# Grouped attention: the values' products move to the last three steps of a tile, copy and join to the next tile's first step, output jobs to two steps behind

## The reference

```python
h = _rms(x, ln_w)
q = (h @ wq).reshape(B, S, 32, 64)          # B*S = 1024 rows in x, causal over all of S
k = (h @ wk).reshape(B, S, 8, 64)
v = (h @ wv).reshape(B, S, 8, 64)
q, k = _rope(q, k)
k, v = jnp.repeat(k, 4, axis=2), jnp.repeat(v, 4, axis=2)
scores = jnp.einsum('bqhd,bkhd->bhqk', q, k) / np.sqrt(64)
attn = jax.nn.softmax(jnp.where(causal, scores, -1e30), -1)
o = jnp.einsum('bhqk,bkhd->bqhd', attn, v).reshape(B, S, 2048)
x = x + o @ wo
```

## Time and profile before

| | |
|---|---|
| median of 3 runs | 3767.97 us (3765.26 to 3775.60) |
| profiled execution | 3772.04 us, span 3770.1 us |
| PE busy | 3251.6 us, 86% |
| DVE busy | 2463.5 us, 65% |
| ACT busy | 1971.1 us, 52% |
| POOL busy | 1694.2 us, 45% |
| layer 0 attention, first scores to the load of its output rows | 107 to 380 us |
| layer 2 attentions, first scores to the final addition L1793 | 1028 to 1698 us, 2459 to 3130 us |

### The profile page before, as it was taken

The page is one execution under the profiler, slowest core; times in us unless marked ns, Lnnn a source line. Parts: engine busy times, 40 slices in busy tenths (PEclk is TensorE's granted clock), DMA queues, the critical chain, the costliest instruction groups (busy, mean ns, idle before and its releaser), DMA issues. The chain is left out here.

```text
span 3770.1 us, 55139 instructions
## 1 busy us (share of the span) xinstructions
PE 3251.6 (86%) x16736; PEld 2534.8 (67%) x16736; DVE 2463.5 (65%) x4877; ACT 1971.1 (52%) x3957; POOL 1694.2 (45%) x1293
## 2 busy tenths in 40 slices
PE   5788698479898989988995999788889988998988
PEld 4566576148566666666883899656666666886767
DVE  4687554965577878875557565378778885555554
ACT  3787433333376767764333333277667774334333
POOL 1676221742366667752212544377666762221111
PEclk8899899889899999999998999899999999999989
DMA  2000231333201111103320000110111103332132
GB/s 76 24 31 2 77 110 61 130 103 116 62 22 28 30 30 29 27 4 122 110 80 26 1 1 1 35 33 25 26 29 32 30 7 101 109 103 93 64 98 73
DMA packets 81187, 204.07 MB, mean 54 GB/s; under 512 B 17179, under 2 KB 20379, under 8 KB 80662
## 3 DMA queue, kind: packets, MB, share of 16 engines
q1 hardware_dynamic: 80774, 200.74, 17.1%
q10 hardware_dynamic: 144, 0.07, 0.0%
HBM read 170.86 MB, written 4.69 MB: 47 GB/s over the span
## 5 line engine op out<-in xcount | busy, mean ns | idle before, releaser
L1253 POOL TENSOR_TENSOR probs<-probs,row_inverse 128x640 f32<-128x640 f32 (+7 forms) x640 | 738.9, 1159 | 485.5 <-DVE row_inverse L1279 474.3
L541 PE MATMUL psUp<-xnT_part,weights_part 128*128 128x512 f32 x3456 | 834.8, 391 | 3.3 <-DVE hidden L694 2.5
L541 PEld LDWEIGHTS psUp<-xnT_part,weights_part 128*128 128x128 f32 x3456 | 651.6, 189 | 141.6 <-POOL weights_part L515 3.3
L518 POOL TENSOR_TENSOR weights_part<-weights,weights_part 128x768 fp32r<-128x768 f32 x136 | 250.9, 1848 | 1010.9 <-ACT weights_part L597 1010.9
L1267 DVE TENSOR_REDUCE neg_max<-psS 128x1 f32<-128x640 f32 (+7 forms) x640 | 476.7, 745 | 134.4 <-PE psS L1157 133.8
L1220 ACT ACTIVATE probs<-psS,neg_max 128x640 f32<-128x640 f32 (+7 forms) x640 | 475.5, 743 | 142.5 <-DVE neg_max L1267 124.7
L1294 DVE TENSOR_TENSOR probsT_part<-psT,probsT_part 128x512 fp32r<-128x512 f32 (+1 forms) x960 | 501.9, 550 | 62.6 <-ACT probsT_part L1236 54.1
L1236 ACT ACTIVATE probsT_part<-psT 128x512 fp32r<-128x512 f32 (+1 forms) x960 | 440.7, 491 | 162.3 <-PE psT L1169 154.0
L1190 PE MATMUL psO<-probsT_part,v_parts 128*128 128x512 f32 x1440 | 441.4, 422 | 76.8 <-DVE probsT_part L1294 76.4
L1169 PE MATMUL psT<-ident,probs 128*128 128x128 f32 x2880 | 445.2, 278 | 46.5 <-DVE probsT_part L1294 44.5
L551 PE MATMUL psDown<-hidden_part,weights_part 128*128 128x512 f32 x1728 | 446.5, 395 | 32.7 <-DVE hidden_part L714 32.7
(11 more groups left out here) (315 smaller groups left out, 4842.1 us busy)
## 6 DMA issues: line engine op xcount, KB each, us to landing
gates<-gate_rows SPq DMA_DIRECT2D x136, 512.0 KB, 4.0
weights<-in_l_ffn SPq DMA_DIRECT2D x148, 384.0 KB, 4.4
qk_swapped<-qk_raw SPq DMA_DIRECT2D x384, 64.0 KB, 2.0
bc_broadcast<-bc_rows SPq DMA_DIRECT2D x32, 512.0 KB, 4.4
w_group<-in_l_wgroup SPq DMA_DIRECT2D x16, 384.0 KB, 3.2
q_whole<-q_steps SPq DMA_DIRECT2D x32, 128.0 KB
w_o_group<-in_l_wo SPq DMA_DIRECT2D x16, 256.0 KB, 2.8
rope<-in_l_rope SPq DMA_DIRECT2D x2, 1024.0 KB, 5.3
```

What stands on the lines that cost most here:

```text
L518: nc.gpsimd.tensor_tensor(w[1][:, j, :], wt[:, j, :], w[0][:, j, :].bitcast(F32), ALU.subtract).then_inc(w_split, 1)
L541: last = nc.tensor.matmul(psU[:, u % 2, g, :], wp[:, j, g * D + k * P:g * D + (k + 1) * P], xp[:, k, cols(half)], start=n == 0, stop=n == ...
L1253: self.nc.gpsimd.tensor_tensor(self.p[:, n % 4, 0:w], self.p[:, n % 4, 0:w], self.rinv[:, at:at + 1].to_broadcast([P, w]), ALU.mult).then_ ...
```

## The change

The values' products of a quad go to its steps 1, 2 and 3 (of 0 to 3) in place of 0, 1 and 2. Copy and join of a quad go from its last step to the first of the next quad; the last quad keeps its step 29 and its join in step 30. Output jobs stand two steps behind the join (the last two quads one), and `oT` becomes two buffers. The projection of step 10 goes to step 11, with the steps of its rotation, swap and addition behind it; rounding and splitting of some pieces and of the next group's values are shifted by a step. Layer 0 gets the first two edits and the steps of the values' rounding.

```diff
--- before.py
+++ after.py
@@ -1122,9 +1122,11 @@
         group(groups - 2, 0, False)
         group(groups - 1, 1, True)
 
-    def joins(self, s):
-
-        return s == 30 or (s > 0 and s % 4 == 3 and s < 31)
+    def joined(self, s):
+
+        if s == self.UNITS - 2:
+            return NT - 1
+        return s // 4 - 1 if s > 0 and s % 4 == 0 else None
 
     def exists(self, n, last):
         return 0 <= n and not (last and n >= self.UNITS)
@@ -1173,11 +1175,10 @@
         def values(g, s, last):
 
             quad, r = s // 4, s % 4
-            if s < 0 or r == 3:
+            if s < 0 or r == 0:
                 return
             blocks = self.blocks(s)
-            lo, hi = (r // 2 if r != 1 else 0, (r + 1) // 2) if blocks == 1 else (
-                r * blocks // 3, (r + 1) * blocks // 3)
+            lo, hi = (0 if r == 1 else 1, 1) if blocks == 1 else ((r - 1) * blocks // 3, r * blocks // 3)
             if lo == 0 and hi > 0:
                 latest = {self.bank(c): c for n in range(4 * quad, 4 * quad + 4) for c in self.chunks(n)}
                 for bank, c in latest.items():
@@ -1222,9 +1223,10 @@
 
         def step(g, s, last):
             exp(g, s + 7, last)
-            if self.joins(s):
-                act.wait_ge(self.valued, NT * g + s // 4 + 1)
-                act.wait_ge(self.kept, NT * g + s // 4 + 1)
+            q = self.joined(s)
+            if q is not None:
+                act.wait_ge(self.valued, NT * g + q + 1)
+                act.wait_ge(self.kept, NT * g + q + 1)
                 nc.scalar.activation(self.shift[:], self.psO[64:64 + self.dv, :], ACT.Copy).then_inc(self.shifted, 1)
             n = s + 4
             if self.exists(n, last):
@@ -1278,11 +1280,12 @@
                 at = n % self.UNITS
                 nc.vector.reciprocal(self.rinv[:, at:at + 1], self.rowsum[:, at:at + 1]).then_inc(self.inverted, 1)
             maximum(g, s + 8, last)
-            if self.joins(s):
-                dve.wait_ge(self.shifted, NT * g + s // 4 + 1)
+            q = self.joined(s)
+            if q is not None:
+                dve.wait_ge(self.shifted, NT * g + q + 1)
                 for half in range(2):
                     pick = lambda ap: ap.rearrange("p (k h w) -> p k h w", h=2, w=P)[:, :, half, :]
-                    done = self.hooks.keep(dve, g, self.tile(s), half, pick(self.psO[0:self.dv, :]),
+                    done = self.hooks.keep(dve, g, self.tile(4 * q), half, pick(self.psO[0:self.dv, :]),
                                            pick(self.shift[:]))
                 done.then_inc(self.kept, 1)
             n = s + 4
@@ -1412,10 +1415,10 @@
             return
         if s in self.SPLIT_AT:
             self.pool_split(pool, g + 1, self.SPLIT_AT[s], lambda: pool.wait_ge(self.att.scaled, 32 * g + s + 7))
-        if s == 28:
+        if s == 29:
             pool.wait_ge(self.att.valued, NT * g + 7)
             self.round_values(g + 1, slice(1, NT))
-        if s == 31:
+        if s == 30:
             pool.wait_ge(self.att.valued, NT * g + 8)
             self.round_values(g + 1, slice(0, 1))
 
@@ -1424,7 +1427,7 @@
             return
         if s == self.FIRST_KEYS_AT:
             self.split_first_keys(dve, g + 1)
-        if s == 29:
+        if s == 30:
             self.split_values(dve, g + 1, 0, slice(1, NT))
         if s == 31:
             self.split_values(dve, g + 1, 1, slice(0, 1))
@@ -1434,8 +1437,10 @@
 
 
 
-    PROJECT = (1, 3, 5, 7, 10, 13)
-    OUTPUT = (4, 8, 12, 16, 20, 24, 28, 31)
+    PROJECT = (1, 3, 5, 7, 11, 13)
+    OUTPUT = (6, 10, 14, 18, 22, 26, 29, 31)
+    ROUND_AT = {6: (0,), 8: (1,), 10: (2,), 12: (3,), 16: (4,), 18: (5,)}
+    SPLIT_AT = {7: 0, 13: 2, 15: 3, 22: 4, 24: 5}
     JOBS = sorted([(s, "project", u) for u, s in enumerate(PROJECT)] + [(s, "output", q) for q, s in enumerate(OUTPUT)])
     UNITS = len(PROJECT)
     VALUES_AT = {-6: (3, 4), -5: (5, 6), -4: (7,)}
@@ -1448,7 +1453,7 @@
         self.rope = s.sb("rope", [P, 2, T])
         self.wp = s.sb("w_group", [P, KD * (D + P)])
         self.wo = s.sb("w_o_group", [P, KD, D])
-        self.oT = s.sb("oT", [P, KD, P])
+        self.oT = [s.sb(f"oT{i}", [P, KD, P]) for i in range(2)]
         self.rot = s.sb("rotated", [P, 2, 2, HALF])
         self.raw = s.sb("qk_raw", [P, 2, HALF])
         self.swap = s.sb("qk_swapped", [P, 2, HALF])
@@ -1576,14 +1581,14 @@
         return done
 
     def keep(self, dve, g, tile, half, first, second):
+        q = GroupAttention.ORDER.index(tile)
         if half == 0:
-            q = GroupAttention.ORDER.index(tile)
-
-            if q:
-                self.wait_filled(dve, g, self.OUTPUT[q - 1], self.last)
+
+            if q > 1:
+                self.wait_filled(dve, g, self.OUTPUT[q - 2], self.last)
             elif not isinstance(g, int) or g:
-                self.wait_filled(dve, g - 1, self.OUTPUT[-1], False)
-        return self.nc.vector.tensor_tensor(self.oT[64 * half:64 * half + 64, :, :], first, second, ALU.add)
+                self.wait_filled(dve, g - 1, self.OUTPUT[NT - 2 + q], False)
+        return self.nc.vector.tensor_tensor(self.oT[q % 2][64 * half:64 * half + 64, :, :], first, second, ALU.add)
 
     def project_values(self, pe, t):
 
@@ -1625,7 +1630,7 @@
             pe.wait_ge(self.wo_loaded, 16 * g + 16)
         pe.wait_ge(self.att.kept, NT * g + j + 2)
         for k in range(KD):
-            done = self.nc.tensor.matmul(self.share(s)[:, 0:D], self.oT[:, k, :], self.wo[:, k, :], start=k == 0,
+            done = self.nc.tensor.matmul(self.share(s)[:, 0:D], self.oT[j % 2][:, k, :], self.wo[:, k, :], start=k == 0,
                                          stop=k == KD - 1)
         done.then_inc(filled, 1)
```

## The result

The changed kernel took 3818.7 us (median; 3815.9 to 3820.0) against 3769.3 of the kernel before on the same chip, ratio 1.0129 with a 95% interval of 1.0111 to 1.0146: 49 us slower. The forecast was 3776, its range ended at 3794. The profiled execution took 3819.3 us, its span 3817.3. The same stretches by windows (length; busy time of PE, PEld, DVE, ACT, POOL; PE's granted clock): a middle group, one behind a back edge, the last one, another middle group, to be held against the earlier trace rows.

What follows compares the result with a forecast made beforehand. PE was taken to set the pace, DVE close behind. Steady groups +17 us in 14 groups, last groups -3, layer 0 -4, back edges -2: sum +8 on the median 3768.0, forecast 3776, range 3748 to 3794.

Steps and rivals of the forecast that it cites:

- The walk of the blocks: Step-by-step estimate of PE's waits in eight four-step blocks of a steady layer 2 group: +0.80 us, with the POOL term +1.2.
- Part (1): Values' products, copy and join later: gains in steps 24-31 and 16-19 (-1.34, -0.56, -0.41), losses elsewhere, most in 4-7 (+1.39).
- (5): POOL's order near steps 13 and 14: DVE's swapped product of step 13 waits 0.4 us for a query split, bounds 0 and 1.3.
- The rival on the slower side: Step 13's swapped product waits for the whole half split, delaying step 14's output job: +1.3 in 14 groups, 3789 us; chance 0.18.
- a rival with the wrong sign: Clock rival: less idle time ahead of four back edges could keep 2.4 GHz, -12 us in all, 3764; chance 0.06.
- a small gain: At the back edges, shorter waits ahead shorten nothing of the 2.56 us idle; -2 us taken for all four.
- part (2): Projection from step 10 to 11: its rotation and copy stand ahead of short step 12, block 12-15 waits +0.86 us.
- Part (3): Output jobs two steps behind with two `oT`: no wait on `oT` ended last, so worth nothing by itself.

Runs made afterwards that it cites:

- a_split_late: The changed kernel with POOL's two query splits of steps 13 and 15 moved to 17 and 18: 3828.5 us, ratio 1.0154.
- a_swap14: The changed kernel with DVE's fifth swapped product moved from step 13 to 14 and POOL's addition one step behind: 3815.1 us, ratio 1.0109.
- a_swap16: The changed kernel with DVE's fifth and sixth swapped products moved from steps 13 and 15 to 14 and 16, POOL's additions one step behind: 3797.7 us, ratio 1.0074.
- b_jobs: The changed kernel with values' products, copy and join back at the steps of before, all other edits kept: 3742.5 us, ratio 0.9922.
- w_mix2: The changed kernel with the values' move only for tiles of steps 24-27, last groups and layer 0, query splits at 12 and 14: 3726.1 us, ratio 0.9889.

## Why the prediction was wrong

**The walk of the blocks held in six of eight.** The recorded terms added to the earlier trace rows, in their order, give 9.26, 8.39, 10.48, 12.66, 11.68, 10.98, 10.53 and 8.14; measured were 9.26, 8.66, 10.47, 12.94, 11.36, 11.84, 11.19 (12.77 with half clock) and 8.25. Six are within 0.33 us; 12-15 and 16-19 are 0.86 and 0.66 too short. Part (1) named the right chain: steps 5 and 13 wait for the exponential behind the copy of the projection (0.49 and 0.60 us), and for the subtraction behind the join (1.09 and 1.21, in the walk 1.40 and 1.51). Last groups gained 2.5 in place of 1.5, layer 0 1.1 for 1.

**The failed term is (5).** The forecast took 0.4 us for one product, between bounds of 0 and 1.3. Two products are held. Freeing the first is worth 0.72 us (`a_split_late`, `a_swap14`), taking the second out of the join's way 0.7 (`a_split_late`, `a_swap16`): 1.4 us a group, so the term was 1.0 too small, 14 us in all. Its premise was a misread trace. The prediction says that the trace of before has no swapped product beside a query split; it has one in each attention, ahead of the groups, and there the product takes 1.67 us, 1.0 more than alone:

```profile
1023.42 2.93 POOL L1571 TENSOR_TENSOR q_parts<-qk_whole,q_parts 64x512 fp32r<-64x512 f32 x2 [0.50 <-ACT q_parts L1554]
1023.56 1.67 DVE L1503 SCALAR_TENSOR_TENSOR rotated<-qk_swapped,rope 128x512 f32<-128x512 f32 x1
```

In before the second product and the split of its step did not meet, because the split of step 14 ran ahead of both; moving that one to 13 freed POOL to begin the other at once. I had looked only at the split whose number the diff changes. The rival on the slower side had the right mechanism at one of its two places. The Trainium skill (SBUF — State Buffer, "Who interferes with whom") has a two-input VectorE instruction and a GpSimd instruction that reads SBUF block each other for a whole instruction. The runs agree but for the last 0.15 us: a product of 0.69 ends 0.54 us behind POOL's instruction whether that is a split or a multiplication, and a pair of splits around one took 2.95 in place of 2.63. I weighed it and took the small end of its range.

**The clock was missing from the sum, and a rival with the wrong sign.** I looked at it only behind back edges; in the middle of a group it had no term. In 8 groups half clock came behind the join's wait in step 16, 1.5 us each; with the groups behind the edges, which took 88 to 93 us, it is a loss where I had a small gain. The Trainium skill (TensorE: Matmul & The Clock Gate, "What's actually happening") ties the throttle to idleness; the rows agree in part: the stretches at half clock read here follow waits of 1.2 to 2.6 us, but in 6 of the 14 groups the same wait went by at full clock.

**The sum.** By the trace the 14 groups took 1224.8 us together in place of 1166.4; the forecast had them at 1166.4 + 14 x 1.2 - 2 = 1181: 44 us, about the whole gap. Middle groups without half clock are 84.0 against 80.9 + 1.2 = 82.1, so 14 x 1.9 = 26. Of these 14 are the held products, 7 are part (2), which was forecast at +0.86 and came out at +1.39 with the product freed (block 12-15 from 9.72 to 11.11), and 5 are small differences of the other blocks. Half clock in block 16-19 is 8 x 1.5 = 12; the remaining 6 lie behind the edges and in the first groups. `a_swap16` took back 21 us of it; what it leaves above the forecast, 22, is about 0.7 x 14 = 10 in the walk and 7 x 1.5 = 10 of half clock. No run had the change without half clock, held products and late POOL work at once, so the closing of this sum is added up from several kernels, and is not shown by one.

**Part (3) was wrong, and hidden.** "No wait on `oT` ended last, so this is worth nothing by itself": it is worth 29 us by the times, 21 to 24 by the groups in the traces. The reason spoke of the buffer, but the edit moved PE work, 0.87 us a job, from behind a wait to a place ahead of DVE's join, and the walk counted the jobs at their new places and booked the gain of blocks 24-27 and 16-19 to the values' move. So what (1) costs together with the hold and the clock that come with it is 76 us, where my terms for (1) come to nothing (-0.06 us a middle group). (A hold of 1.3 us stands in `b_jobs` too; without it, in `w_mix2`, block 12-15 is 0.6 us shorter.) The forecast of the whole was not hurt by that, but whoever had chosen edits by it would have kept the wrong one.

**Shown and not shown.** Shown: the gain of the jobs alone, the cost of the values' move in tiles with projections, its gain elsewhere, the hold of two products and its size. Not tested: a third product, that of step 7, lasts 1.15 us beside a split of keys in place of 0.81; the blocks around it came out near the forecast. Not shown: what decides whether a wait is followed by half clock. It moved from steps 17 and 18 to step 13 when the wait of step 16 was shortened, and no kernel separates the length of one wait from those around it.

## What to carry to other kernels

Cost each edit of a change alone as well as the whole: a buffer that nobody waits for can still come with an order that is the largest gain of the change. Move the tail of a tile under the next one's work only where something on PE stands over it; here it paid in tiles without projections and cost up to 1.7 us a block in the others. And when a change shifts an engine's steps by a microsecond, look again at every pair of VectorE and POOL instructions with SBUF operands in the stretch, not only at those whose line was edited, and search the whole trace for such a pair, the part ahead of the loop too, before guessing its price.

## What the runs showed of the hardware

Half clock set in with PE at work again, within 1.2 us of the end of a wait of 1.91 to 1.95 us, in 8 of 14 groups with the same instructions and the same wait; with that wait shortened to 0.87 it came in another step, in 7 groups. A product of VectorE with two SBUF operands took 1.76 us in place of 0.69 beside a single multiplication of POOL of 1.68 that had begun ahead of it and was not lengthened; where the two began together, the product took its 0.68 and POOL's instruction 1.16 in place of 0.61.
